# Prologue of a cross-attention and mixture-of-experts kernel: weight loads reordered, identity products ahead of the weight folds, value fold ahead of the transposes, query fold copied on ScalarE

## The reference, cut to what matters

```python
        x1 = layernorm(modality1, ln1_g, ln1_b)
        x2 = layernorm(modality2, ln2_g, ln2_b)
        q = x1 @ Wq + bq
        k = x2 @ Wk + bk
        v = x2 @ Wv + bv
        scores = jnp.einsum('bqe,bke->bqk', q, k) * scaling
        attn = jax.nn.softmax(scores, axis=-1)
        ctx = jnp.einsum('bqk,bke->bqe', attn, v)
        return ctx @ Wo + bo
...
        shared = _gelu(x @ ws1 + bs1) @ ws2 + bs2
        aff = jax.nn.softmax(x @ Wr + br, axis=-1)
        vals, idx = jax.lax.top_k(aff, K)
...
            h = _gelu(x @ W1 + B1)
            return (acc + g[..., None] * (h @ W2 + B2), None)
...
        return shared + routed + x
```

## Time and profile before

| | us |
|---|---|
| median of 3 runs | 521.79 (520.79 to 525.07) |
| the profiled execution | 525.94 |
| its span, first to last instruction | 524.2 |
| PE busy | 476.3 (91%) |
| DVE busy | 351.1 (67%) |
| POOL busy | 323.1 (62%) |
| ACT busy | 247.7 (47%) |
| mean granted TensorE clock | 0.966 of full speed |

### The profile page before, as it was taken

How to read it: one execution, slowest core, us unless ns; L and a number is a source line. 1 busy time by engine, 2 the same in 40 slices (tenths; PEclk the granted TensorE clock), 3 DMA queues, 4 the chain that set the end, 5 groups by cost and what they waited for, 6 DMA issues and landing times.

```text
span 524.2 us, 13549 instructions
## 1 busy us (share of the span) xinstructions
PE 476.3 (91%) x3204; PEld 416.1 (79%) x3204; DVE 351.1 (67%) x1556; ACT 247.7 (47%) x821; POOL 323.1 (62%) x363
## 2 busy tenths in 40 slices
PE   0989889899898998998799999999999999999992
PEld 0777778677677786777689889999999999989992
DVE  3748788786877858556756766666666666662584
ACT  1255555555464643646345444545455555543220
POOL 6123757766567665456428888878888888785000
PEclk9989998998899987999999999999999999999998
DMA  7364756676665992159449999989888898885999
GB/s 235 98 216 144 223 188 200 224 216 217 189 198 179 307 292 91 60 192 309 179 101 183 183 186 188 190 154 143 138 136 137 135 144 140 128 133 60 334 348 320
DMA packets 80621, 97.53 MB, mean 186 GB/s; under 512 B 8689, under 2 KB 65298, under 8 KB 80546
## 3 DMA queue, kind: packets, MB, share of 16 engines
q1 hardware_dynamic: 60786, 70.79, 44.8%
q0 software_dynamic: 19472, 25.61, 29.4%
q10 hardware_dynamic: 288, 0.27, 0.3%
HBM read 54.91 MB, written 41.73 MB: 184 GB/s over the span
## 4 chain that ended last, share of the span: by engine, by line
PE 70%; DVE 9%; SPq 4%; issue 3%; DMA 2%; ACT 1%; POOL 0%; DVEq 0%; another core or an unknown queue 0%; POOLq 0%
PE bank L1184 18%; PE bank L1195 18%; PE bank L1173 4%; PE bank L1051 3%; PE bank L1039 3%; PE bank L1040 3%; PE bank L1054 2%; PE bank L1077 2%; PE bank L1026 2%; PE bank L1078 2%; DVE w_all L732 2%; PE bank L1069 2%; DMA w_all<-sum 2%; PE bank L1071 1%; PE bank L988 1%
## 5 line engine op out<-in xcount | busy, mean ns | idle before, releaser
L557 POOL DMA_INDIRECT sum<-y_sb,token x105 | 168.3, 1603 | 49.9 <-issue 24.1
L643 ACT ACTIVATE up<-bank,b_all 128x128 f32<-128x128 f32 x260 | 81.6, 364 | 102.0 <-PE bank L1184 45.9
L1184 PE MATMUL bank<-xtt,w1b 128*128 128x128 f32 x840 | 111.3, 275 | 0.3 <-ACT xtt L669 0.3
L1195 PE MATMUL bank<-w_all,up 128*128 x420 | 109.2, 382 | 0.1
L1184 PEld LDWEIGHTS bank<-xtt,w1b 128*128 128x128 f32 x840 | 102.1, 192 | 1.0 <-ACT xtt L669 0.5
L921 DVE TENSOR_SCALAR y_sb<-bank,gate,inverse 128x256 f32<-128x256 f32 x105 | 57.1, 544 | 53.3 <-PE bank L1195 31.4
L535 POOL DMA_INDIRECT expert_rows_in<-xt,slot x75 | 76.2, 1017 | 26.2 <-issue 20.9
L1195 PEld LDWEIGHTS bank<-w_all,up 128*128 128x128 f32 x420 | 71.7, 191 | 6.3 <-issue 0.5
L913 DVE COPY w1b<-w_all 128x512 f32 x105 | 48.1, 458 | 19.6 <-issue 7.6
L669 ACT ACTIVATE xtt<-bank 128x256 f32<-128x256 f32 x105 | 40.2, 384 | 39.5 <-issue 20.0
L1173 PE MATMUL bank<-ident,xt 128*128 128x128 f32 x210 | 40.1, 274 | 0.2 <-issue 0.2
(11 more groups left out here) (180 smaller groups left out, 947.3 us busy)
## 6 DMA issues: line engine op xcount, KB each, us to landing
xt<-expert_rows_in SPq DMA_DIRECT2D x105, 132.0 KB
w_all<-in_w SPq DMA_DIRECT2D x47, 256.0 KB
...
```

Of the source, the lines that this page charges most:

```text
L557: pool.indirect_dma_start(sums[s], bass.IndirectOffsetOnAxis(ap=token[sx][:, 0:1], axis=0), y_sb[sx][:, :], None, compute_op=ALU.add).then ...
L643: ins = act.activation(up[s][:, m * P:m * P + P], up_ps[s][:, m * P:m * P + P], ACT.Gelu, bias=b1_all[:, e, m:m + 1].rearrange("p o n -> p ...
L1184: mm = pe.matmul(up_ps[s][:, m * P:m * P + P], w[:, c * INTER + m * P:c * INTER + m * P + P], xtt[s][:, c * P:c * P + P], start=(c == 0), ...
L1195: mm = pe.matmul(down_ps[s], up[s][:, m * P:m * P + P], w, start=(m == 0), stop=(m == 1))
```

## The change

The diff touches the prologue alone.
1. SP loads the key and query weights first, on a semaphore of their own (`query_weights_in`), then token tile 0, context batch 0, and the value and output weights (`value_weights_in`).
2. POOL makes the identity first (constant number 4), and issues no more small loads; ACT issues them: three as soon as the key and query sums are there, four behind the copy of `fold_q`.
3. DVE makes the key and query sums first, step(-2) behind them, and the value sums behind that.
4. PE begins with 22 products of the identity with itself into a bank that nobody reads.
5. PE makes the value fold ahead of the transposes of tile 0 and batch 0, not behind the first queries.
6. The copy of `fold_q` out of PSUM moves from DVE to ACT; its constant factor is now folded into `g1_s` by one small DVE instruction.

```diff
 
-        weights_in, cols_in, small_in, made, shared_in, expert_in = sems(
-            "weights_in", "cols_in", "small_in", "made", "shared_in", "expert_in")
+        query_weights_in, value_weights_in, cols_in, small_in, made, shared_in, expert_in = sems(
+            "query_weights_in", "value_weights_in", "cols_in", "small_in", "made", "shared_in", "expert_in")
         x_in = sems(*[f"x_in{s}" for s in range(8)])
...
 
+            sp.dma_start(wk_aug[:, :, 0:D2], wkt.rearrange("(c p) e -> p c e", p=P)).then_inc(query_weights_in, 16)
+            sp.dma_start(wqt_s[:, :, :], wqt.rearrange("(c p) e -> p c e", p=P)).then_inc(query_weights_in, 16)
+            load_x(0)
             load_ctx(0)
-            load_x(0)
-            for dst, src in (
-                (wk_aug[:, :, 0:D2], wkt.rearrange("(c p) e -> p c e", p=P)), (wqt_s[:, :, :], wqt.rearrange("(c p) e -> p c e", p=P)),
-                (wv_aug[:, :, 0:D2], wvt.rearrange("(c p) e -> p c e", p=P)),
-                (wo_s[:, :, :], wo.rearrange("(c p) e -> p c e", p=P)), (bo_row[D2B:D2C, :], bo),
-            ):
-                sp.dma_start(dst, src).then_inc(weights_in, 16)
+            sp.dma_start(wv_aug[:, :, 0:D2], wvt.rearrange("(c p) e -> p c e", p=P)).then_inc(value_weights_in, 16)
+            sp.dma_start(wo_s[:, :, :], wo.rearrange("(c p) e -> p c e", p=P)).then_inc(value_weights_in, 16)
+            sp.dma_start(bo_row[D2B:D2C, :], bo).then_inc(value_weights_in, 16)
             load_ctx(1)
...
             const(pool.memset(mhalf[:, :], -0.5))
+            const(pool.memset(ident[:, :], 0.0))
+            k = const(pool.memset(tri[:, :], 1.0))
+            pool.wait_ge(made, k)
+            k = const(pool.affine_select(out=ident[:, :], in_=ident[:, :], compare_op=ALU.not_equal, fill=1.0,
+                                         base=0, pattern=[[-1, P]], channel_multiplier=1))
+            assert k == IDENT_MADE, k
             const(pool.memset(eps_cols[:, 0:3], EPS))
             const(pool.memset(eps_cols[:, 3:4], EPS * EPS / (1.0 + EPS)))
             for s in range(SLOTS):
                 const(pool.memset(z[s][:, :, D2:D2 + 1], 1.0))
-            const(pool.memset(ident[:, :], 0.0))
-            k = const(pool.memset(tri[:, :], 1.0))
-            pool.wait_ge(made, k)
-            const(pool.affine_select(out=ident[:, :], in_=ident[:, :], compare_op=ALU.not_equal, fill=1.0,
-                                     base=0, pattern=[[-1, P]], channel_multiplier=1))
             const(pool.affine_select(out=tri[:, :], in_=tri[:, :], compare_op=ALU.is_gt, fill=0.0,
...
             alone(pool)
-
-            pool.dma_start(wr_s[:, :, :], wr.rearrange("(c p) e -> p c e", p=P)).then_inc(small_in, 16)
-            pool.dma_start(br_s[:, :], br.partition_broadcast(P)).then_inc(small_in, 16)
-            pool.dma_start(b1_all[:, :, :], be1).then_inc(small_in, 16)
-            for q in range(4):
-                pool.dma_start(b2_all[q * 32:q * 32 + NE + 1, q, :], b2).then_inc(small_in, 16)
 
...
             act.activation(negtop[0][:, :], mhalf[:, 0:1], ACT.Exp)
+            act.wait_ge(made, MADE)
+            act.wait_ge(aug_ready, 2)
+            alone(act)
+            act.dma_start(wr_s[:, :, :], wr.rearrange("(c p) e -> p c e", p=P)).then_inc(small_in, 16)
+            act.dma_start(br_s[:, :], br.partition_broadcast(P)).then_inc(small_in, 16)
+            act.dma_start(b1_all[:, :, :], be1).then_inc(small_in, 16)
+            act.wait_ge(cols_in, 16 * 2)
+            act.wait_ge(folds_made, 1)
+            for a in range(2):
+                ins = act.activation(fold_q[:, a, :], bank[7][:, a * 256:a * 256 + D2 + 1], ACT.Copy, scale=g1_s[:, a:a + 1])
+            ins.then_inc(fold_q_ready, 1)
+            for q in range(4):
+                act.dma_start(b2_all[q * 32:q * 32 + NE + 1, q, :], b2).then_inc(small_in, 16)
 
...
             dve.wait_ge(made, MADE)
-            step(-2)
-
             dve.wait_ge(cols_in, 16 * 2)
             dve.memset(g2_1[D2B:D2C, :], 1.0).then_inc(dve_chain, 1)
             dve.memset(fold_o0[:, D1:D1 + 1], 0.0).then_inc(dve_chain, 1)
             dve.memset(fold_o1[0:D2B, D1:D1 + 1], 0.0).then_inc(dve_chain, 1)
             dve.memset(fold_o1[D2B:D2C, D1:D1 + 1], 1.0).then_inc(dve_chain, 1)
-            dve.wait_ge(weights_in, 16 * 5)
+            dve.tensor_scalar(g1_s, g1_s, (1.0 + EPS) ** -0.5, None, ALU.mult)
+            dve.wait_ge(query_weights_in, 16 * 2)
             for c in range(2):
                 dve.tensor_tensor_reduce(bank[0][:, c * D2:c * D2 + D2], wk_aug[:, c, 0:D2], b2_row, 1.0, bk_s[:, c:c + 1], ALU.mult, ALU.add,
                                          wk_aug[:, c, D2:D2 + 1])
             for c in range(2):
                 dve.tensor_tensor_reduce(bank[1][:, c * D1:c * D1 + D1], wqt_s[:, c, :], b1_row, 1.0, bq_s[:, c:c + 1], ALU.mult, ALU.add,
                                          uq[:, c:c + 1]).then_inc(aug_ready, 1)
+            step(-2)
+            dve.wait_ge(value_weights_in, 16 * 3)
             for c in range(2):
...
             dve.tensor_scalar(qs1[:, 0:1], g2_1, SCALE, None, ALU.mult).then_inc(dve_chain, 1)
-            dve.wait_ge(folds_made, 1)
-            for a in range(2):
-                ins = dve.tensor_scalar(fold_q[:, a, :], bank[7][:, a * 256:a * 256 + D2 + 1], g1_s[:, a:a + 1],
-                                        (1.0 + EPS) ** -0.5, ALU.mult, ALU.mult)
-            ins.then_inc(fold_q_ready, 1)
             dve.wait_ge(dve_chain, 6)
...
 
+            pe.wait_ge(made, IDENT_MADE)
+            for k in range(22):
+                pe.matmul(bank[6][:, 0:P], ident[:, :], ident[:, :], start=True, stop=True)
             pe.wait_ge(made, MADE)
...
             mm.then_inc(folds_made, 1)
+            pe.wait_ge(aug_ready, 4)
+            for c in range(2):
+                pe.matmul(bank[5][:, 0:D1], wv_aug[:, c, 0:P], wo_s[:, c, :], start=(c == 0), stop=(c == 1))
+            for c in range(2):
+                mm = pe.matmul(bank[5][0:D2C, D1:2 * D1], wv_aug[:, c, P:D2 + 1], wo_s[:, c, :], start=(c == 0), stop=(c == 1))
+            mm.then_inc(folds_made, 1)
             turn_x(0)
             turn_ctx(0)
-
-            def value_folds():
-                pe.wait_ge(aug_ready, 4)
-                for c in range(2):
-                    pe.matmul(bank[5][:, 0:D1], wv_aug[:, c, 0:P], wo_s[:, c, :], start=(c == 0), stop=(c == 1))
-                for c in range(2):
-                    mm = pe.matmul(bank[5][0:D2C, D1:2 * D1], wv_aug[:, c, P:D2 + 1], wo_s[:, c, :], start=(c == 0), stop=(c == 1))
-                mm.then_inc(folds_made, 1)
 
...
                 step(i)
-                if i == 0:
-                    value_folds()
                 if i == 1:
```

1 line of the change is left out of this document (added).

## The result

| | before | after |
|---|---|---|
| median of 4 runs | 521.77 (520.79 to 525.07) | 516.47 (512.48 to 517.22) |
| the profiled execution | 525.94 | 517.22 |
| its span | 524.2 | 515.6 |
| PE busy | 476.3 | 473.5 |
| DVE busy | 351.1 | 349.8 |

The medians are 5.3 us apart, which is 1.0%. The ratio on record is 0.986, with an interval of 0.9817 to 0.9903; it is not the quotient of these two medians (0.990, which lies inside the interval), and by it the gain is 1.4%. The forecast was 517.2 and, as the likeliest outcome, "within 1%". The time is 0.7 us from the forecast and inside the range, but the interval excludes "no change" and the ratio lies beyond 1%: the class is not the one forecast.

What follows compares the result with a forecast made beforehand. The prologue was bound by weights landing, DVE's list, PE's value fold, then DVE's list again. DVE's step(1) at 18.9 against 23.53 gives 4.6 us, so 521.79 - 4.6 = 517.2, range 514.5 to 520.5.

Steps and rivals of the forecast that it cites:

- Landing of the query weights: Prologue loads: query weights, first on SP's queue, land at 7.2 us (bounds 6.6 and 8.0), letting DVE's sums start.
- DVE's list: DVE's prologue work after the landing: value sums at 10.6, step(1) at 18.9 against 23.53, 4.6 us sooner.
- PE: Prologue products and folds on PE: covered either way, scores about 20.3, ahead of DVE's need at 21.2.
- the late end: Identity products on PE: end near 11 if the clock rises late, near 8.3 if soon; the late case was taken.
- ACT and POOL: Prologue: ACT's loads and fold copy (10.6 to 11.4) hidden, 1.0 us to spare; POOL's first power at 12.0, no wait.
- The new wait for POOL's power: DVE's step(0) in the prologue: waiting for POOL's power adds 0.3 us, giving 17.5 instead of 17.2.
- The rule on pauses: PE's prologue pauses: the skill warns the clock falls between bursts; by it the products buy only the fold.
- rival 2: Less gain, 519 to 519.5: clock falls again ahead of step(2) (1.7 us), or tables or weights land late; chance 0.18.
- Carry: From prologue to end: a shift in the hand-over's start is carried one for one, as each phase waits for the last.
- rival 4: Nothing changes, 521 to 522: something that does not move, as a transfer, takes up the shift; chance 0.06.
- Rival 1: More gain, 515.5: the low clock in the first full step, worth some 1.7 us, falls away or shifts; chance 0.20.
- the last step, from the gain to the class: End result: measurement tells about 1% (5.2 us) from no change, so 0.61 for "within 1%", 0.37 for faster.

Runs made afterwards that it cites:

- products_only: The kernel before with the identity made first and the 22 identity products, nothing else changed; one run, 501.13 beside 503.66 for before.
- fold_q_on_dve: The changed kernel with the copy of the query fold moved from ACT back to DVE; one run, 498.24 beside 503.66 for before.
- delay: The changed kernel with eight reductions (4.84 us) on DVE ahead of its first sums; 521.91 us, ratio to before 1.0008.
- small_on_pool: The changed kernel with the seven small loads back on POOL's queue; one run, 495.96 beside 503.66 for before.
- after_third: The changed kernel unchanged, run in a later set on a faster chip; 498.9 against 502.72 for before, ratio 0.9927.
- after_fourth: The changed kernel unchanged, on another chip than after_third; 499.69 against 503.26 for before, ratio 0.995.
- value_late_again: The changed kernel with PE's value fold back behind the first queries, second set; 500.37 beside 499.69 for after_fourth, ratio to before 0.995.
- after_again: The changed kernel unchanged, measured again with 10 runs; 515.65 against 519.04 for before, ratio 0.9924.
- before_again: The kernel before, unchanged, profiled again on one chip together with after_fifth; 522.51 us.
- after_fifth: The changed kernel unchanged, profiled on one chip together with before_again; 518.35 us.

## Why the prediction was right, and where it was wrong

**Landing of the query weights: right.** 7.2 was forecast, 7.25 measured, inside 6.6 to 8.0; over all profiles of the new order it lay between 7.08 and 7.81. What I treated as fixed was the other end: the last of the five weights is in at 10.21 in one run of before, at 9.82 in another and at 9.36 in products_only, so the gain of this term is 1.6 to 3.1 us, where the forecast had 3.0 with a range from 2.2 to 3.6. One sum in it is off: half of 3.1 us ahead of 10.2 gives 8.65, not 8.0, as the late bound; with it the least gain of the whole is 3.15 and not 3.8.

**DVE's list: right.** Value sums 10.6 forecast and 10.33 measured, step(1) 18.9 and 18.83. Two parts are worth 3 us each, the wait that fell away (2.97 us ahead of L857) and the new landing; step(-2), which now stands behind the first sums, takes 1.6 of it back. The two copies that moved to ACT gave 0.55 of DVE time in the trace of fold_q_on_dve, 0.73 in the sum.

**PE: right on what DVE waits for.** The query fold at 9.03 in 1.54 (forecast: 9, in 1.5), L1031 at 22.40 (22.5). The products end at 8.86, nearer the early than the late end: 6.97 us for 44 instructions at 0.21 and 0.11 makes about 21 of them slow, so the level rose near 6.4. Taking the late end cost nothing, as all of it was covered. Undone one by one, the products carry 0.5, the value fold's place 1.4 to 1.5, the order of the loads 1.1 to 1.2, the copy 0.55, the small loads nothing, and the shorter wait (two loads, not five) 1.05 to 1.9: together 4.6 to 5.7 against the 4.1 to 4.7 seen, since some of these cover each other.

**ACT and POOL: right.** 10.68 against 10.6, and no wait for loads in the place of the removed ones. The new wait for POOL's power, 0.3 in the sum, is some 0.15 of idle time ahead of L740 in each of two steps. The small loads land 2 to 3 us behind their issue, not 5.2; that was hidden either way.

**The rule on pauses.** The granted clock is 0.50 in the window 23:24, behind a pause of 2.40 us, and 0.50 in 12:18 of products_only, behind one of 2.63. In the changed kernel the fold behind a pause of 0.16 was fast, and in delay, behind 5.08, slow. But in small_on_pool the level is 1.00 in the same window 23:24, behind the same 2.40. The Trainium skill ("TensorE: Matmul & The Clock Gate", section "HAM oscillation — how this bites in real kernels") says that the clock falls in pauses between bursts and that each burst then starts cold. The traces agree in part: delay's folds are its case, in products_only the burst started fast and the level fell behind its start, and in small_on_pool it did not fall. The consequence that the prediction drew for the sum, rival 2, did not come: the level is low in step(2) of before as well, so this price stands on both sides of the difference.

**Carry: right, one for one through the loop.** after_third and after_fourth keep their 0.5 to 0.6, fold_q_on_dve keeps its 2.2 behind small_on_pool, value_late_again 1.06 of 1.35. delay takes the whole gain away (6.05 later at step(2), 6.3 in the medians, 4.4 by the ratios), and rival 4 is out. Behind the loop a shift of this size can't be followed in single executions, for the scatter there.

**Rival 1 was half right and not for its reason.** Its price for a low step 2, 1.7 us, is what the traces show (6.70 against 5.03). In the first pair a low stretch of 3.9 us is missing after the change. But it lies in step 28 and not in step 2, the changed kernel has longer ones in after_again (its time 522.22), and the pair before_again and after_fifth has hardly any of this difference. It is scatter of both kernels.

**What failed is the last step, from the gain to the class.** It reads: "The measurement tells about 1% from no change, 5.2 us here", and so puts 0.61 on "within 1%" although the sum itself forecasts 4.6 us. Two terms of it were mis-sized. The first is what the measurement can tell: the interval came out as 0.43% to either side, 2.2 us, and 0.3% in the three later comparisons; all four exclude no change (0.9817 to 0.9903, 0.9893 to 0.9956, 0.9902 to 0.9953, 0.992 to 0.9981). A gain of 4.6 us was to be seen as one. The second is the scatter, for which the range had one microsecond. Single runs of after lie between 512.1 and 522.2 on one chip and those of before between 516.1 and 527.1; by an estimate from these runs (drawing four at random from each) the difference of two medians of four scatters by 2 us, and by 1 us on the two faster chips. Low stretches that come and go between runs, and the scatter behind the loop, had no place in the sum, although the profiled execution of before lay 4.15 above its median; and the profiled execution of after, 517.22 where 521.3 was forecast, owes 3.9 of these 4.1 us to the one step 28.

The four comparisons with several runs of both gave 5.3, 3.4, 3.8 and 3.6 us by the medians, and ratios of 0.986, 0.9924, 0.9927 and 0.995: three of four within 1%, and the one that the forecast was made for beyond. By the same estimate the difference comes out beyond 5.2 us once in five such comparisons; that it is told from no change is what the sum itself implied. The median 0.7 us from the forecast is in part luck as well, with a scatter of 1.5 us in a median of four (the same estimate). The mechanism and the sizes in the prologue held. The direct evidence of the size is the traces, 4.07 and 4.70 at step(2), and it should have been stated as 4.1 to 4.7, since the 10.21 of one profile was only the late end of its term.

**What stays open.** Whether products in later pauses gain anything, and whether the change would be better without its own (514.6 without, 515.65 with, intervals that overlap); why the loop has low stretches in three sets and none in the profiles of three others; why a step without a low stretch is shorter there; what decides whether the level falls behind a pause of 2.40 us; what makes the expert tiles take up to 3 us more in one execution than in another; and by what the 0.5 us wait for `slotf` in step 6 was removed.
